# Loading the linear attention's tokens for two units in one transfer of 256 KB

## The reference

```python
x = x + window_attention(group_norm(x))        # 7x7 shifted windows, 4 heads
t = x.reshape(16, 3136, 128)
# linear attention, causal, per image
q, k, v = split(layer_norm(t) @ W.T + b); q = elu(q) + 1; k = elu(k) + 1
kv_cum, k_cum = cumsum(k outer v), cumsum(k)
t = t + (q @ kv_cum) / (q . k_cum + 1e-6)
# recurrence over the 3136 tokens
w = batch_norm(layer_norm(t) @ Wf.T) * gamma + beta
y_i = sigmoid(w_i + y_(i-1) @ V.T)
t = t + y
```

## Time and profile before

| | |
|---|---|
| runs | 1857.97, 1854.97, 1857.34 us, median 1857.34 |
| profiled execution | 1857.33 us, span 1855.5 us |
| PE busy | 1823.2 us (98%) |
| DVE busy | 1523.3 us (82%) |
| ACT busy | 1215.8 us (66%) |
| POOL busy | 1011.1 us (54%) |
| loads `la_xc<-x` (L743) | 196, 128 KB each, median 2.1 us from issue to landing |
| stores `t<-la_tn` (L749) | 196, 129 KB each, median 2.3 us |

### The profile page before, as it was taken

One profiled execution on the slowest core, in us unless ns is written; L12 is line 12 of the kernel. 1 busy time (PEld: TensorE's weight loads), 2 busy tenths in 40 slices (PEclk: granted clock), 3 DMA queues, 4 the chain that ended last, 5 costly groups with the idle time before them and its releaser, 6 DMA issues.

```text
span 1855.5 us, 57715 instructions
## 1 busy us (share of the span) xinstructions
PE 1823.2 (98%) x19600; PEld 1616.4 (87%) x19600; DVE 1523.3 (82%) x4705; ACT 1215.8 (66%) x3180; POOL 1011.1 (54%) x1177
## 2 busy tenths in 40 slices
PE   7999999999999999899999999999999998999998
PEld 6888888888888888799999999999999998888886
DVE  7888888888888888688888888888888887566665
ACT  5877888888888887566666666666666665333333
POOL 6878888888888888533333333333333434432321
PEclk9999999999999999999999999999999999999999
DMA  5333334333333332122222222222223222556543
GB/s 170 104 100 107 106 106 106 107 106 105 104 106 104 103 83 79 46 70 69 69 67 68 70 67 67 70 65 70 66 69 93 67 70 83 210 178 221 188 166 126
DMA packets 207109, 187.02 MB, mean 101 GB/s; under 512 B 14577, under 2 KB 190945, under 8 KB 206817
## 3 DMA queue, kind: packets, MB, share of 16 engines
q1 hardware_dynamic: 205664, 182.14, 33.1%
q10 hardware_dynamic: 1152, 1.13, 0.2%
HBM read 105.95 MB, written 77.27 MB: 99 GB/s over the span
## 4 chain that ended last, share of the span: by engine, by line
PE 54%; issue 27%; POOL 16%; DVE 1%; DMA 1%; POOLq 0%; ACT 0%; ACTq 0%; DVEq 0%; SPq 0%
POOL la_rstd L983 11%; PE k_psum L343 7%; PE k_psum L293 6%; PE k_psum L286 6%; PE k_psum L311 6%; PE k_psum L327 5%; PE k_psum L359 5%; PE k_psum L1393 5%; PE k_psum L1384 5%; PE k_psum L277 4%; POOL la_spread L977 3%; PE k_psum L1374 2%; PE k_psum L1401 2%; POOL la_tn L988 2%; POOLq L39 0%
## 5 line engine op out<-in xcount | busy, mean ns | idle before, releaser
L977 POOL TENSOR_SCALAR la_spread<-la_mv 128x4 f32<-128x4 f32 (+1 forms) x203 | 46.2, 227 | 483.2 <-DVE la_mv L1083 483.1
L606 POOL TENSOR_TENSOR wa_prob<-wa_prob,wa_peak 128x784 f32<-128x784 f32 x128 | 194.8, 1522 | 115.3 <-DVE wa_peak L477 115.3
L924 ACT ACTIVATE la_ve<-k_psum 128x256 f32<-128x256 f32 x196 | 75.6, 385 | 231.9 <-PE k_psum L807 231.9
L983 POOL TENSOR_TENSOR la_rstd<-la_spread,k_exponent 128x4 f32<-128x4 f32 (+1 forms) x203 | 207.7, 1023 | 17.2 <-POOL la_spread L977 0.4
L1458 ACT ACTIVATE sc_y<-k_psum,sc_cols 128x256 f32<-128x256 f32 x207 | 98.2, 474 | 178.6 <-PE k_psum L1393 178.6
L795 PE MATMUL k_psum<-la_uT,la_wt 128*128 128x256 f32 x784 | 202.5, 381 | 0.0
L613 POOL TENSOR_TENSOR wa_prob<-wa_prob,wa_inv 128x784 f32<-128x784 f32 x128 | 195.1, 1524 | 11.3 <-DVE wa_inv L438 11.3
L1039 DVE SCALAR_TENSOR_TENSOR la_fqk<-k_psum,la_raised 128x512 f32<-128x512 f32 x196 | 135.5, 691 | 77.4 <-ACT la_raised L916 77.3
L1184 POOL TENSOR_TENSOR sc_ub<-sc_tb 128x3584 f32<-128x3584 f32 (+6 forms) x22 | 92.9, 4223 | 174.6 <-PE k_psum L1374 173.2
L469 DVE TENSOR_TENSOR wa_prob<-k_psum,wa_bias 128x784 f32<-128x784 f32 x128 | 124.9, 976 | 66.5 <-PE k_psum L311 66.3
L916 ACT ACTIVATE la_raised<-k_psum,la_minus_one 128x512 f32<-128x512 f32 x196 | 134.8, 688 | 44.2 <-PE k_psum L795 44.0
(11 more groups left out here) (134 smaller groups left out, 5298.8 us busy)
## 6 DMA issues: line engine op xcount, KB each, us to landing
t<-la_tn SPq DMA_DIRECT2D x196, 129.0 KB, 2.3
la_xc<-x SPq DMA_DIRECT2D x196, 128.0 KB, 2.1
wa_xT<-in_x_cm SPq DMA_DIRECT2D x124, 196.0 KB, 3.4
sc_tb<-t SPq DMA_DIRECT2D x12, 1806.0 KB, 8.8
out<-sc_ob SPq DMA_DIRECT2D x12, 1792.0 KB, 12.6
wa_xw<-in_x_tok SPq DMA_DIRECT2D x64, 224.0 KB, 2.8
wa_xw<-in_x_tok SPq DMA_DIRECT2D x64, 168.0 KB, 2.4
x<-wa_y SPq DMA_DIRECT2D x64, 168.0 KB, 2.9
```

The source lines that it names most:

```text
L606: nc.gpsimd.tensor_tensor(s, s, peak[:, k % S, :].unsqueeze(2).broadcast_to([128, PAIRS * HEADS, WIN]), ALU.subtract).then_inc(lowered, 1)
L983: nc.gpsimd.tensor_tensor(rstd[:, n % S, used], spread[:, used], exponent[:, used], ALU.pow).then_inc(rooted, 1)
```

## The change

An even n loads unit n and unit n+1 in one transfer of 256 KB into two neighbouring slots; an odd n loads nothing. The wait on `attended` is that of unit n+1, since its slot is overwritten too, and the image that must have been stored is that of the last token of the pair. The statistics of both units wait on the semaphore of the even slot.

```diff
--- before.py
+++ after.py
@@ -734,13 +734,14 @@
                 yield
 
                 def load(n):
-                    if not inside(n, UNITS):
-                        return
-                    last = (n * 2 * P + 2 * P - 1) // T
+                    if not inside(n, UNITS) or n % 2:
+                        return
+                    last = (n * 2 * P + 4 * P - 1) // T
                     if n == 0 or last != (n * 2 * P - 1) // T:
                         await_image(last)
-                    at_least(sp, attended, n - XS + 1)
-                    sp.dma_start(xc[:, n % XS], rows(x1, n)).then_inc(loaded[n % XS], 16)
+                    at_least(sp, attended, n + 1 - XS + 1)
+                    pair = x1.rearrange("b t c -> (b t) c")[n * 2 * P:(n + 2) * 2 * P, :].rearrange("(u a p) c -> p u a c", u=2, p=P)
+                    sp.dma_start(xc[:, n % XS:n % XS + 2], pair).then_inc(loaded[n % XS], 16)
 
                 def store(n):
                     if not inside(n, UNITS):
@@ -1062,7 +1063,7 @@
                     if not inside(n, ROWS):
                         return
                     if inside(n, UNITS):
-                        dve.wait_ge(loaded[n % XS], (n // XS + 1) * 16)
+                        dve.wait_ge(loaded[(n - n % 2) % XS], (n // XS + 1) * 16)
                     if inside(n - AHEAD, UNITS):
                         dve.wait_ge(attended, n - AHEAD + 1)
                     for which, tile, m in ((0, xc, n), (1, tn, n - AHEAD)):
```

## The result

The changed kernel takes 2007.02 us (median of four runs, 1997.36 to 2025.15) against 1856.65 before: a ratio of 1.082, with a 95% interval of 1.078 to 1.086. Forecast were 1969 us and a range of 1927 to 2035. So the direction and the range held, and of the rise, 150 us, the forecast had 112. The profiled execution took 2010.04 us, its span is 2007.9.

The account below looks back on a forecast made before the run. TensorE was taken to set the linear attention's pace, VectorE a close second. Exposed landings make a pair 9.15 us instead of 7.96; 94 x 1.19 = 112 us on 1857 gives 1969 us, range 1927 to 2035.

Parts of the forecast that it names:

- The margin and the release: Linear attention's loads: pair released one unit later, 2.1 us margin becomes a stall once per two units, 94 times.
- The loop over a pair: Linear attention, release to release: 4.42 + 3.03 + 0.03 + 1.67 = 9.15 us against 7.96, losing 1.19 a pair.
- third wait: Pair loop: VectorE's own loop takes 9.09 us, close to 9.15, so no further wait should hide in between.
- The landing, L = 2.7: 256 KB load, issue to landing: 2.54 us undisturbed, 2.7 taken; each 0.1 us is 9.4 us of the run.
- The row of 224 KB at 2.8: Earlier trace's window-token loads, always followed closely by other transfers, landing in 2.8 us; cited for taking L as 2.7.
- Rival 2: 256 KB load: second half nearly free, L = 2.1, loss 0.59 us a pair, 1913 us; chance 5%.
- Rival 1: 256 KB load crowded by the two stores behind it: landing 3.4 us, loss 1.89 a pair, 2035 us; chance 12%.
- One L for all pairs: Linear attention's sum: the same landing of 2.7 us for all 94 waiting pairs, 94 x 1.19 = 112 us.
- rival 5: TensorE, 87% busy, gets the 1.2 GHz clock; held all stage, some 780 us more, about 2640 us; chance 5%.
- Rivals 3, 4 and 6: Stall absorbed (3) or pair still early (6): 1857 us, 3% together; 98 issues come back (4): 35 us, 1822 us, 2%.

Follow-up runs that it names:

- the size without the wait: Changed kernel with ten slots for the tokens instead of eight, so the 256 KB pair waits for unit m-9 instead of m-7: 1857.31 us, ratio 1.000.
- a_two: Changed kernel with two 128 KB transfers issued where the pair's wait ends, each unit waiting for its own semaphore: 1921.72 us, ratio 1.036.
- the one with the fill: Changed kernel plus five unused matmuls of ones on TensorE ahead of its once-per-pair wait for `combine`: 1998.67 us, ratio 1.077.
- h_strict_single: Kernel before, 128 KB loads, each load waiting one unit longer than it has to (unit m-7 instead of m-8): 2108.26 us, ratio 1.137.

## Why the prediction was right, and where it was short

- **The margin and the release.** Right: 94 stalls, as counted, and both halves of it shown, by the wait without the size (+65 us) and the size without the wait (none).
- **The loop over a pair.** Right: 9.15 us for a pair whose load landed as assumed, piece by piece within 0.12 us, and the loop moved as it should when its release, its reader or its number was changed (three experiments). TensorE was at 88 of 100 us, 87 forecast. No third wait closed.
- **The landing, L = 2.7.** Mis-sized, a term of the sum: the median is 2.9. Over the stage this is 9.29 - 9.15 = 0.14 us a pair, 13 us. The step that failed is the addition of 0.44 us for the second 128 KB at the peak rate of 299 GB/s; with the store right behind it gone it still took 0.7 more than the 2.1 of the earlier trace rows. In the kernel with two transfers of 128 KB (`a_two`) the first lands in 2.1 us in the median, as before, and the second, issued 0.4 us after it, in 2.4: the pair is there after 2.8 us, about as with one transfer. So the second 128 KB take 0.7 to 0.8 us and not 0.44. The row of 224 KB at 2.8 was the better guide. Rival 2 (the second half free) is out. Rival 1's landing of 3.4 did not come, and of its reason the half that was tried, the store right behind the load, did next to nothing.
- **One L for all pairs.** This is the larger miss. The sum took a median landing for each of 94 loads, but with no slack left the mean counts: eleven late pairs add 29 us over their medians. The spread was in the earlier trace rows (2.1 in the median, 3.1 at most) and, for a load behind other transfers, in the earlier trace rows (4.2). It cost nothing there, for 2.1 us of margin lay above it and TensorE had slack for the rest.
- **The lower clock** (rival 5). It came, but not as the rival had it: not for the stage, in six short drops after late landings, 1.6 to 2.1 us each, some 10 of the 29 us. A drop isn't decided by the length of the idle time alone: VectorE's waits of 4.28, 4.49 and 4.54 us had none, one of 3.80 had. The Trainium skill (page "TensorE: Matmul & The Clock Gate", its section on oscillation) says that waits for DMA between groups of matmuls let the clock fall again each time; the trace agrees for six pairs of 94, with TensorE idle for 2.25 to 3.60 us before the drop, and not for five others, idle for 2.19 to 2.99, nor for the ordinary gap of 1.1 us (the median).
- Together: 112 + 13 + 29 = 154 us, against 152.7 in the profiled execution (2010.04 less 1857.33). The 29 are this execution's: in the traces of the kernel with the store first and of the one with the fill, late pairs add 20 and 4 us. That 2007 lies within the range is in part luck: its upper end was drawn for a landing of 3.4 us on every load (rival 1), and what filled it were late landings and the clock, to which the sum gave nothing.
- **Rivals 3, 4 and 6.** None: no stall was absorbed whole, and the 98 issues saved are worth nothing (1857.31 us with ten slots).

## What to carry to other kernels

When transfers are merged, ask first when the last of the merged buffers comes free, not how many bytes go at once: the group waits for its last slot and is needed by its first reader, so the margin shrinks by one unit for each one merged beyond the first. With N slots and groups of two, either give two slots more, or place the release early and the reader late in the step; both gave the whole 150 us back here, where the earlier release alone gave 64. And where a transfer's time becomes exposed, price it with the mean and the tail, not the median, and with what the engine behind it does when it stands idle.

## What the runs showed of the hardware

- From SyncE's queue, in rows of 512 bytes, 256 KB land in 2.9 us in the median (2.6 to 5.3) and 128 KB in 2.1 (2.0 to 4.2, by the kernel before): 0.8 us for the second 128 KB. In the kernel with ten slots, where a store of 129 KB goes out 0.4 us ahead, 256 KB take 3.6.
- The landings have a long tail: 11 of the 94 that wait took 4.0 us or more. In each an instruction-code transfer started within 3 us of the issue, as it did for 15 of the other 83; in the case shown a trickle of some 19 GB/s stood at the end. What holds that last part was not tried.
- TensorE's clock fell to 1.2 GHz for a few microseconds (some 3.3 in the case shown) after some of its longer idle gaps: six of 2.25 to 3.60 us had a drop, five of 2.19 to 2.99 had none, in a stage in which it was busy for about 88 us of 100. Each such drop went with 1.6 to 2.1 us more. With every unit delayed (`h_strict_single`) it fell six times too, after gaps of 1.8 to 2.1 us.
